# Last self attention of a twelve-stage decoder kernel: ScalarE's exponentials of a unit ahead of its casts of the next group's queries

## The chip, the cores and the metric

One core of a Trainium2 chip runs the whole program in one launch. The metric is the device time in microseconds. The kernel before took 1790.76 us in the median of three runs (1790.09, 1790.76, 1799.61). The program is four decoder layers of three sublayers each (self attention, cross attention or a stand-in for it, feed-forward), on a residual of 4 batches of 256 tokens of 256 features.

## The reference

The change lies in the self attention of the last layer: 16 heads of 16 features, causal, on the layer-normalised residual. The other eleven sublayers are the same in both kernels.

```python
def _L3_attn_ref(x, w_qkv, b_qkv, w_out, b_out):
    qkv = x @ w_qkv + b_qkv
    q, k, v = jnp.split(qkv, 3, axis=-1)
    q, k, v = (heads(q), heads(k), heads(v))        # b, 16 heads, 256 tokens, 16
    scores = jnp.einsum('bhql,bhkl->bhqk', q, k) / math.sqrt(HEAD)
    scores = jnp.where(q_ind < k_ind, jnp.float32(-10000.0), scores)
    probs = jax.nn.softmax(scores, axis=-1)
    combined = jnp.einsum('bhqk,bhkl->bhql', probs, v)
    combined = combined.transpose(0, 2, 1, 3).reshape(b, s, HIDDEN)
    return combined @ w_out + b_out

x = x + _L3_attn_ref(_layernorm(x, axis=-1), ...)
```

## The kernel before

Each of twelve stages is a function (`l0_attention` to `l3_ffn`) that returns five Python generators, one for each engine's queue: TensorE `t`, VectorE `v`, ScalarE `a`, GpSimd `g`, SyncE `sp`. The order in which a generator issues instructions is the order in that engine's queue. `yield signal, key` asks for the count of a semaphore at which a step is done, and `wait_ge` on it makes the engine wait; every instruction behind it in the same queue waits too. `yield MEET` is a barrier of all engines. One stands at the end of the stage `l3_attention` and at its beginning.

The stage works on 16 groups m of four heads in one batch (group m has batch m // 4), each of two units of two heads: unit u belongs to group u // 2, and there are UNITS = 32. All five generators run over the same iterations n = 0 to 41 (`LAST = UNITS + 10`), and in iteration n each engine does its step for a unit that is some iterations behind. There is no other scheduler: the order inside an iteration is written out by hand.

The queries and keys are split into three bf16 parts whose sum carries the float32 value. A pair of iterations begins a group: in the even iteration n the group n // 2 is projected (`qkv_tensor` on TensorE, L101) and moved out of PSUM with its bias (`qkv_vector` on VectorE, L2779 and L2780). ScalarE casts the first part of the queries in the same even iteration, the second part in the odd one and the third part in the next even one (`parts_scalar`, L2579, called with 0, 1 and 2); VectorE casts the keys likewise (`parts_vector`, L2569), and after each cast GpSimd takes the part from what is left (`parts_gpsimd`, L2586 and L2588), for which the next cast waits.

For unit u the steps are, with the iteration in which each is issued:
- n = u + 3: TensorE turns the parts of queries and keys (`narrow_turns_tensor`, L107, bf16 identity). VectorE copies an odd unit's result (L2881) in the same iteration, ScalarE an even unit's (L2920).
- n = u + 4: TensorE makes the scores of both heads (`narrow_scores_tensor`, L2616, L2617 and L2619; L2617 fills the masked block). The scores of the units go round three PSUM banks, so the second head of unit u needs the bank that the first head of unit u - 1 held, and waits until its exponentials are done (`score_bank_free` with the signal `exped`). VectorE masks and takes the maxima (`masked_maxima`, L2842, L2844, L2846, the last being the negated maximum). ScalarE takes the exponentials, four instructions with their sums (`exponentials_scalar`, L585, waiting for `neg_max`, and for a buffer and the sums of earlier units).
- n = u + 5: VectorE inverts the sums (`sums_vector`, L597), GpSimd multiplies (`shares_gpsimd`, L605).
- n = u + 6: TensorE turns the shares (`share_turns_tensor`, L107, float32 identity). In n = u + 7 VectorE copies the first head's (L543) and ScalarE the second head's (L550).
- n = u + 8: TensorE multiplies with the values (`heads_tensor_of_pair`, L2800). For an even unit of a later group it first waits for ScalarE's copy of the group before (`heads_copied`, L2808, issued in the even iteration 2m + 10).
- For each batch, in n = 17, 25, 33 and 41, TensorE makes the output product (L101) and VectorE adds it to the residual (L403) and takes statistics.

Besides these, VectorE works for the next stage in n = 9, 13 (its weights as integers) and 21, 29, 37 (its activations), ScalarE copies weights in n = 12 and 16 (L2731, L2732) and normalises a batch in n = 19, 27 and 35 (L367), for which GpSimd has made the scale in n = 18, 26 and 34 (L328 to L340).

TensorE's order in an iteration is: turns of n - 3, scores of n - 4, heads of n - 8, projection (even n), output product, turns of the shares of n - 6. VectorE's: copy of the shares' turn, copy of the queries' turn (even n), maxima, inverted sums, cast of the third part (even n), projection's bias (even n), cast of the first or second part, output, work for the next stage.

Of the kernel before, what the change touches and what calls it, by code (L numbers as in the profile page):

```python
# [44 lines left out]
UNITS = GROUPS * NB * 2  # L45
# [85 lines left out]
def build(nc, d, out):  # L131
# [442 lines left out]
    def exponentials_scalar(A, n, src_of=score_bank):  # L574
        k = n % 2
        for hh in range(2):
            e, src = A.eb[(2 * n + hh) % len(A.eb)], src_of(n, hh)
            a.wait_ge(*(yield neg_max, A.s, n, hh))
            if n >= A.depth:
                a.wait_ge(*(yield p_in_psum, A.s, n - A.depth, hh))  # L580
            if n >= 2:
                a.wait_ge(*(yield vs, A.s, "sums", n - 2))
            for i in range(TB):
                c = slice(A.ko[i], A.ko[i] + A.kw[i])
                ins = a.activation(e[:, c], src[:, c], ACT.Exp, bias=A.mx[k][:, 2 * hh + i:2 * hh + i + 1], scale=A.scale,  # L585
                                   accum_out=A.ls[k][:, 2 * hh + i:2 * hh + i + 1])
            ins.then_inc(*exped.up(A.s, n, hh))
# [1984 lines left out]
    def parts_scalar(N, m, n):  # L2572
        cur, q5 = N.current(m, n), slots(N.qx[m % 2])
        if n:
            a.wait_ge(*(yield rest_of, N.A.s, m, n - 1))
        lo, hi = Q_SLOTS[n]
        for i in range(TB):
            src = cur[:, i, 0:64].rearrange("p (h o c) -> p h o c", h=HG, o=1)
            ins = a.copy(q5[:, i, :, lo:hi, :], src.broadcast_to([P, HG, hi - lo, HD]))  # L2579
        ins.then_inc(*part_a.up(N.A.s, m, n))  # L2580
# [153 lines left out]
    def l3_attention():  # L2734
# [10 lines left out]
        A = Attention(s, BF16, HD, HD ** -0.5, False, outs=(), q_cols=1024, depth=3)  # L2745
# [156 lines left out]
        def scalar():  # L2902
            yield from norm_scalar(s, nf, None, [3], both=True)
            for n in range(LAST):
                if n == 1:
                    yield from turned_scalar(s, 3, heads_bank)
                if n - 3 in WEIGHTS:
                    yield from cross_weights_scalar(A, WEIGHTS.index(n - 3))
                if n in (19, 27, 35):
                    yield from norm_scalar("l3x", cross_nf, None, [(n - 19) // 8], both=True)  # L2910
                if 0 <= n - 10 < UNITS and n % 2 == 0:
                    yield from heads_copied((n - 10) // 2)
                if 0 <= n - 7 < UNITS:
                    yield from probability_turns_scalar(A, n - 7)
                if 0 <= n - 3 < UNITS and n % 2:
                    u = n - 3
                    a.wait_ge(*(yield q_in_psum, s, u))
                    if u >= 2:
                        a.wait_ge(*(yield scored, s, u - 2, 1))
                    a.copy(*narrow_turned(N, u)).then_inc(*q_t_a.up(s, u))  # L2920
                if 0 <= n - 1 < UNITS and n % 2 == 0:
                    yield from parts_scalar(N, n // 2 - 1, 2)
                if n < UNITS and n % 2 == 0:
                    a.wait_ge(*(yield vs, s, "qkv", n // 2))
                    yield from parts_scalar(N, n // 2, 0)
                if n < UNITS and n % 2:
                    yield from parts_scalar(N, n // 2, 1)
                if 0 <= n - 4 < UNITS:
                    yield from exponentials_scalar(A, n - 4)
            yield MEET  # L2930

        def gpsimd():
# [406 lines left out]
```

## Time and profile before

| what | value |
|---|---|
| runs before | 1790.09, 1790.76, 1799.61 us; median 1790.76 |
| the profiled execution | 1797.26 us |
| its span, first to last instruction | 1795.9 us |
| instructions | 27080 |
| mean granted TensorE clock | 0.85 of full |
| busy in the whole span | TensorE 1496.4 us (83%), VectorE 1144.2 (64%), ScalarE 818.3 (46%), GpSimd 765.6 (43%) |

The stage of the change runs from about 1226 us of the span, where its pipeline begins, to about 1432 us, where the next stage's first instructions follow the barrier. The shares of busy time in the table are means over twelve stages with different limits and say little on this one.

In the profile's rows PE is TensorE, DVE is VectorE, ACT is ScalarE, POOL is GpSimd. L585 is line 585 of the kernel. A row of a timeline is an instruction or several like it, and in brackets the idle time of the engine ahead of it, with what ended that time; "issue" stands where no releaser is seen.

### The profile page before, as it was taken

Reading aid. Unit: us, or ns where it says so; the run is one execution under the profiler, and the core shown is the slowest. Engines: PE = TensorE matmul, PEld = TensorE weight load, DVE = VectorE, ACT = ScalarE, POOL = GpSimd, SP = SyncE. Lnnn points to the kernel's source line nnn. Section 1 sums busy time; section 2 is a strip of 40 time slices with the busy share of each in tenths; the row PEclk is TensorE's granted clock in tenths of the full one; section 3 lists DMA queues with packets and bytes.
Section 4 is the critical chain, followed back from the end, with each engine's and each line's share of the span. In section 5 each row is a group of like instructions: output and inputs, shape, how many; then the busy total and the mean of one; then the engine's idle time right before and its main releaser. Section 6 shows DMA issues by size and latency. Waiting matters only on the chain. (4 is left out here: it accounts for less than half of the span.)

```text
span 1795.9 us, 27080 instructions
## 1 busy us (share of the span) xinstructions
PE 1496.4 (83%) x8792; PEld 1110.0 (62%) x8792; DVE 1144.2 (64%) x2987; ACT 818.3 (46%) x2138; POOL 765.6 (43%) x1199
## 2 busy tenths in 40 slices
PE   3899997899999948999898694166777689959999
PEld 3567673578888822333476584035555479958888
DVE  2577786255555569988555526886888579963222
ACT  1244443134444338887515313456665468832111
POOL 3388882046555646666422204275455322220000
PEclk8799997799999975555599897587989879968999
DMA  5100000200000025555420000200000020000000
GB/s 218 56 7 7 1 2 12 100 14 6 7 1 1 1 53 92 95 89 94 123 99 1 1 1 27 84 16 1 1 1 1 35 108 2 2 1 1 7 6 12
DMA packets 98379, 62.21 MB, mean 35 GB/s; under 512 B 88896, under 2 KB 93376, under 8 KB 96448
## 3 DMA queue, kind: packets, MB, share of 16 engines
q1 hardware_dynamic: 98240, 60.48, 12.6%
q8 instruction: 72, 1.18, 0.3%
q14 instruction: 67, 0.55, 0.1%
HBM read 38.44 MB, written 1.05 MB: 22 GB/s over the span
## 5 line engine op out<-in xcount | busy, mean ns | idle before, releaser
L101 PE MATMUL banks<-normed_t,arena_a 128*128 128x256 f32 x1120 | 258.9, 387 | 3.0 <-PEq L3244 3.0
L101 PEld LDWEIGHTS banks<-normed_t,arena_a 128*128 128x128 f32 x1120 | 217.1, 195 | 34.7 <-issue 4.1
L446 POOL TENSOR_TENSOR lut_weights<-lut_weights,arena_b 128x536 f32<-128x536 f32 x128 | 179.5, 1402 | 123.8 <-DVE arena_b L436 114.0
L605 POOL TENSOR_SCALAR work<-work,small 128x256 f32<-128x256 f32 (+1 forms) x384 | 175.5, 475 | 85.5 <-DVE small L597 85.2
L101 PE MATMUL banks<-arena_a 64*128 64x512 bf16 (+1 forms) x384 | 161.6, 540 | 30.8 <-PEq L3244 18.7
L1615 ACT ACTIVATE arena_a<-banks,work 128x1024 uint8<-128x1024 f32 x128 | 154.1, 1205 | 47.1 <-DVE work L1553 40.5
L1551 DVE TENSOR_REDUCE work<-banks 128x1 f32<-128x1024 f32 x128 | 155.3, 1214 | 24.3 <-PE banks L101 24.3
L1645 POOL TENSOR_SCALAR arena_a<-arena_a 128x1024 bf16<-128x1024 uint8 x128 | 132.2, 1045 | 65.1 <-DMA arena_a<-arena_a 64.6
L107 PE MATMUL banks<-identity,work 128*128 128x128 f32 x968 | 136.9, 283 | 19.4 <-ACT work L550 7.4
L585 ACT ACTIVATE work<-banks,small 128x256 f32<-128x256 f32 (+1 forms) x258 | 115.3, 458 | 62.5 <-DVE small L572 58.7
L107 PEld LDWEIGHTS banks<-identity,work 128*128 128x128 f32 x968 | 116.2, 149 | 34.8 <-POOL work L605 12.7
L1741 DVE TENSOR_TENSOR big_b<-big_b,banks 128x512 f32<-128x512 f32 (+2 forms) x48 | 30.8, 642 | 148.2 <-PE banks L101 128.0
L328 POOL TENSOR_SCALAR rstd<-mean_var 128x2 f32<-128x2 f32 x48 | 10.1, 209 | 245.3 <-DVE mean_var L399 163.5
L1757 ACT ACTIVATE big_b<-banks 128x512 f32<-128x512 f32 (+2 forms) x48 | 26.7, 560 | 176.7 <-PE banks L101 176.6
L101 PEld LDWEIGHTS bank<-work,arena_a 128*128 128x128 bf16 x1024 | 37.2, 106 | 110.8 <-POOL arena_a L1645 75.7
L101 PE MATMUL banks<-arena_a,normed_t 128*128 128x192 f32 (+2 forms) x320 | 100.2, 465 | 3.5 <-PEq L3244 3.5
L2579 ACT CAST big_a<-big_b 128x192 bf16<-128x192 f32 (+1 forms) x192 | 55.3, 340 | 76.6 <-DVE big_b L2779 48.3
L101 PE MATMUL bank<-big_b,work 128*128 128x16 f32 (+2 forms) x596 | 84.4, 279 | 0.4 <-DVE work L543 0.3
L101 PEld LDWEIGHTS banks<-arena_a,normed_t 128*128 128x128 f32 x320 | 58.5, 217 | 36.9 <-issue 35.9
L101 PEld LDWEIGHTS bank<-big_b,work 128*128 128x128 f32 x596 | 75.2, 198 | 5.7 <-DVE work L543 3.9
L101 PE MATMUL bank<-arena_a,big_b 128*128 128x256 f32 x288 | 70.2, 388 | 4.6 <-DVE big_b L2035 2.8
L101 PEld LDWEIGHTS banks<-arena_a 64*128 64x128 bf16 (+1 forms) x384 | 39.6, 134 | 55.3 <-issue 35.2
(403 smaller groups left out, 3401.9 us busy)
## 6 DMA issues: line engine op xcount, KB each, us to landing
arena_a<-in_L3f_wg SPq DMA_DIRECT2D x1, 4096.0 KB, 12.6
arena_b<-in_lut_idx SPq DMA_DIRECT2D x8, 268.0 KB, 3.2
arena_b<-in_L_wqn SPq DMA_DIRECT2D x1, 2048.0 KB, 12.0
arena_b<-in_L_wo SPq DMA_DIRECT2D x1, 2048.0 KB, 17.8
arena_a<-in_L_wq SPq DMA_DIRECT2D x1, 2048.0 KB, 7.6
arena_a<-in_L_wo SPq DMA_DIRECT2D x1, 2048.0 KB, 13.0
arena_a<-arena_a SPq DMA_TRANSPOSE x128, 2.5
arena_b<-in_L2f_gv SPq DMA_DIRECT2D x1, 2048.0 KB, 8.3
```

Of the source, the lines that this page charges most:

```text
L101: ins = t.matmul(out, lhs_t, rhs, start=start and i == 0, stop=stop and i == n - 1)
L107: ins = t.transpose(out, src, ident[0:src.shape[0], 0:src.shape[0]])
L328: g.tensor_scalar(dst, src, factor, more, ALU.mult, ALU.add).then_inc(*gs.up())
L446: g.tensor_tensor(o, o, lut_t[j % 2], ALU.add).then_inc(*summed.up(c * LUT + j))
L585: ins = a.activation(e[:, c], src[:, c], ACT.Exp, bias=A.mx[k][:, 2 * hh + i:2 * hh + i + 1], scale=A.scale, accum_out=A.ls[k][:, 2 * hh + ...
L605: ins = g.tensor_scalar(e[:, c], e[:, c], A.rl[n % 2][:, 2 * hh + i:2 * hh + i + 1], 0.0, ALU.mult, ALU.add)
L1551: v.tensor_reduce(mx[:, z:z + 1], wide[n % 3], AX.X, ALU.max).then_inc(*vs.up())
L1615: a.activation(eb[n % 6].bitcast(U8), wide[n % 3], ACT.Exp, bias=mx[:, n:n + 1], scale=sq[:, n:n + 1], accum_out=ls[:, n:n + 1]).then_inc( ...
L1645: g.tensor_scalar(pt[n % 6].rearrange("p (j e q) -> p j e q", j=NT // 2, e=2), by_byte(p8[n % 6]), 1.0, 0.0, ALU.mult, ALU.add).then_inc(* ...
L1741: ins = v.tensor_tensor(o[r, cols], o[r, cols], (banks[q % 3 * 2].f if r.start else up)[r, cols], ALU.mult)
L1757: ins = a.activation(F.hidden(q)[dst, cols], banks[q % 3 * 2].f[src, cols], ACT.Silu)
L2579: ins = a.copy(q5[:, i, :, lo:hi, :], src.broadcast_to([P, HG, hi - lo, HD]))
```

## The change

In ScalarE's generator of this stage, in every iteration, the exponentials of unit n - 4 move from the end of the iteration to a place ahead of the cast of the first part (even n, with its wait for VectorE's projection) or of the second part (odd n). They stay behind the copies of turned shares and queries and behind the cast of the third part. No instruction, wait, buffer or DMA is added or taken away, and the other engines' queues are as they were.

```diff
@@ -2920,13 +2920,13 @@
                     a.copy(*narrow_turned(N, u)).then_inc(*q_t_a.up(s, u))
                 if 0 <= n - 1 < UNITS and n % 2 == 0:
                     yield from parts_scalar(N, n // 2 - 1, 2)
+                if 0 <= n - 4 < UNITS:
+                    yield from exponentials_scalar(A, n - 4)
                 if n < UNITS and n % 2 == 0:
                     a.wait_ge(*(yield vs, s, "qkv", n // 2))
                     yield from parts_scalar(N, n // 2, 0)
                 if n < UNITS and n % 2:
                     yield from parts_scalar(N, n // 2, 1)
-                if 0 <= n - 4 < UNITS:
-                    yield from exponentials_scalar(A, n - 4)
             yield MEET
 
         def gpsimd():
```

ScalarE's queue in n = 22 and 23 (L2808, L550, L2579 x32: copy of the heads, copy of the shares' turn, cast of the third part; then L2579 x48, first part, L585, the exponentials of unit 18; from the second L550 on n = 23), before:

```order
L2808 COPY big_a<-bank 128x256
L550 COPY work<-banks 128x512
L2579 CAST big_a<-big_b 128x4x32 x2
L2579 CAST big_a<-big_b 128x4x48 x2
L585 ACTIVATE work,small<-banks,small 128x256 x4
L550 COPY work<-banks 128x512
L2920 COPY work<-banks 128x1024
L2579 CAST big_a<-big_b 128x4x48 x2
L585 ACTIVATE work,small<-bank,small 128x256 x2
L585 ACTIVATE work,small<-banks,small 128x256 x2
```

and with the change:

```order
L2808 COPY big_a<-bank 128x256
L550 COPY work<-banks 128x512
L2579 CAST big_a<-big_b 128x4x32 x2
L585 ACTIVATE work,small<-banks,small 128x256 x4
L2579 CAST big_a<-big_b 128x4x48 x2
L550 COPY work<-banks 128x512
L2920 COPY work<-banks 128x1024
L585 ACTIVATE work,small<-bank,small 128x256 x2
L585 ACTIVATE work,small<-banks,small 128x256 x2
L2579 CAST big_a<-big_b 128x4x48 x2
```

In both iterations the row L585 and the cast L2579 128x4x48 have changed places: in n = 22 the exponentials are behind the third part's cast, in n = 23 behind the copy of the turned queries (L2920), and the heads' copy of n = 24, which comes next in the queue, now follows the cast of the second part.

ScalarE's queue in n = 4 and 5, the first iterations with exponentials, before:

```order
L2579 CAST big_a<-big_b 128x4x32 x2
L2579 CAST big_a<-big_b 128x4x48 x2
L585 ACT_TABLE_LOAD
L585 ACTIVATE work,small<-banks,small 128x256 x4
L2920 COPY work<-banks 128x1024
L2579 CAST big_a<-big_b 128x4x48 x2
L585 ACTIVATE work,small<-bank,small 128x256 x2
L585 ACTIVATE work,small<-banks,small 128x256 x2
```

and with the change:

```order
L2579 CAST big_a<-big_b 128x4x32 x2
L585 ACT_TABLE_LOAD
L585 ACTIVATE work,small<-banks,small 128x256 x4
L2579 CAST big_a<-big_b 128x4x48 x2
L2920 COPY work<-banks 128x1024
L585 ACTIVATE work,small<-bank,small 128x256 x2
L585 ACTIVATE work,small<-banks,small 128x256 x2
L2579 CAST big_a<-big_b 128x4x48 x2
```

The load of the table for the exponential moves with the first of them, ahead of the cast of group 2's first part.

## Rows read from the trace of the kernel before

**Rows 1.** Waits of ScalarE, 1226 to 1414 us: total us, times, longest
```profile
ACT big_a L2579 <- DVE big_b L2779: 48.3, 15, 5.7
```

**Rows 2.** Waits of VectorE, 1226 to 1414 us, same columns
```profile
DVE residual L403 <- PE banks L101: 6.7, 3, 2.4
...
DVE work L2881 <- PE banks L107: 5.7, 6, 2.3
...
DVE big_b L2779 <- PE banks L101: 4.9, 4, 3.0
```

**Rows 3.** Windows: us; busy us (count) of PE, PEld, DVE, ACT, POOL; clock; DMA
```profile
1236.00:1414.00 178.00, 135.09 (x1050) 97.99 (x1050) 148.98 (x422) 115.06 (x397) 91.70 (x191) 0.89 0.00 1
...
1370.00:1382.00 12.00, 10.28 (x75) 7.28 (x73) 8.09 (x24) 7.78 (x30) 3.59 (x9) 0.72 0.00 0
```

**Rows 4.** Timeline, n = 22 to 24: start us, duration us, engine, line, operation
```profile
1338.38 0.17 DVE L2846 TENSOR_SCALAR small<-small 128x2 f32<-128x2 f32 x1
...
1339.65 0.17 DVE L2846 TENSOR_SCALAR small<-small 128x2 f32<-128x2 f32 x1
...
1340.26 0.61 PE L107 MATMUL banks<-identity_bf,big_a 128*128 128x128 bf16 x8 [1.40 <-issue]
...
1340.52 0.61 ACT L2579 CAST big_a<-big_b 128x192 bf16<-128x192 f32 x2 [4.05 <-DVE big_b L2779]
...
1341.03 0.47 ACT L585 ACTIVATE work<-banks,small 128x256 f32<-128x256 f32 x1
...
1342.10 0.23 PE L2616 MATMUL banks<-work 128*128 128x128 bf16 x1 [1.02 <-ACT work L585]
...
1342.84 0.59 ACT L550 COPY work<-banks 128x512 f32<-128x512 f32 x1
...
1344.21 0.64 ACT L2579 CAST big_a<-big_b 128x192 bf16<-128x192 f32 x2
...
1344.25 0.17 DVE L2846 TENSOR_SCALAR small<-small 128x2 f32<-128x2 f32 x1
...
1344.61 1.92 POOL L605 TENSOR_SCALAR work<-work,small 128x256 f32<-128x256 f32 x4 [1.72 <-DVE small L597]
...
1345.28 0.69 DVE L543 COPY work<-banks 128x512 f32<-128x512 f32 x1 [0.45 <-PE banks L107]
...
1346.53 0.42 ACT L2808 COPY big_a<-bank 128x256 f32<-128x256 f32 x1
...
1346.62 0.69 DVE L2881 COPY work<-banks 128x1024 bf16<-128x1024 bf16 x1 [0.65 <-PE banks L107]
```

**Rows 5.** Timeline, VectorE, its other waits in the stage
```profile
1240.03 0.43 DVE L2842 COPY_PREDICATED banks<-arena_b 128x256 f32<-128x256 int32 x1 [1.68 <-PE banks L2619]
...
1278.29 0.43 DVE L2779 TENSOR_TENSOR big_b<-banks,arena_a 128x256 f32<-128x256 f32 x1 [1.10 <-PE banks L101]
...
1298.37 0.69 DVE L543 COPY work<-banks 128x512 f32<-128x512 f32 x1 [2.20 <-PE banks L107]
...
1357.20 0.69 DVE L403 TENSOR_TENSOR residual<-banks,residual 128x512 f32<-128x512 f32 x1 [2.35 <-PE banks L101]
...
1377.25 0.42 DVE L2779 TENSOR_TENSOR big_b<-banks,arena_a 128x256 f32<-128x256 f32 x1 [3.03 <-PE banks L101]
...
1394.22 0.69 DVE L543 COPY work<-banks 128x512 f32<-128x512 f32 x1 [0.61 <-PE banks L107]
```

**Rows 6.** Timeline, ScalarE and TensorE: the start, n = 15 and n = 25
```profile
1236.39 0.60 ACT L2579 CAST big_a<-big_b 128x192 bf16<-128x192 f32 x2 [2.02 <-DVE big_b L2779]
...
1237.01 1.28 ACT L585 ACT_TABLE_LOAD   x1
...
1239.38 0.29 PE L2616 MATMUL banks<-work 128*128 128x128 bf16 x1 [2.43 <-ACT work L585]
...
1293.44 0.29 PE L2616 MATMUL bank<-work 128*128 128x128 bf16 x1 [0.40 <-ACT work L585]
...
1352.13 0.23 PE L2616 MATMUL banks<-work 128*128 128x128 bf16 x1 [0.94 <-ACT work L585]
```

## Prediction

> **What bounds the kernel now.** The change touches one stage, the last self attention, from about 1226 to 1432 us of the span. It is a software pipeline of 42 iterations (n = 0 to 41), and no engine is full in it: between 1236 and 1414 us VectorE is busy 149.0 of 178 us (84%), TensorE's matmuls 135.1, ScalarE 115.1, GpSimd 91.7 [rows 3]. So the stage goes at the pace of VectorE plus whatever VectorE waits for. I read the waits in two views. ScalarE waits longest at its first cast of a group's queries, for VectorE's projected queries: 15 times, 48.3 us [rows 1]. That is the wait in front of the moved exponentials, but idle time of an engine with a third to spare costs nothing by itself. VectorE's own list is what counts: 6.7 us for the output products (L403), 5.7 us for turned queries (L2881), 4.9 us for projections (L2779), all behind TensorE [rows 2].
>
> The timeline of n = 22 to 24 shows how the two lists hang together [rows 4]. VectorE has negated the maxima of the even unit's two heads at 1338.55 and 1339.82. ScalarE sits in the cast's wait (4.05 us) until 1340.52, starts the first exponential at 1341.03 and only then frees a score bank; TensorE waits 1.02 us for that (1342.10), and comes late to the heads, the turned shares and the turned queries. VectorE waits for these two turns: 0.45 us at 1345.28 and 0.65 us at 1346.62.
>
> **What the change does to one pair.** The four exponentials of a unit (1.81 us, 1341.03 to 1342.84, accumulator reads in it [rows 4]) go ahead of the cast. Nothing is added or removed; no DMA, no queue of SP and nothing on GpSimd moves. Even iteration: first head from 1338.55 to about 1339.45, second from 1339.82 to 1340.72, inside the 4.05 us. The cast then starts at 1340.72 instead of 1340.52, 0.2 us late. It feeds GpSimd's remainder, and GpSimd is busy with shares at that time, as it is at 1344.61 in the row of the odd iteration, so I cost it at nothing. TensorE's second head finds its bank free: its 1.02 us is gone.
>
> Odd iteration: ScalarE's copies (L550, 1342.84 before) come some 1.6 us sooner. The exponentials now stand ahead of the cast of the second parts, and wait for the maxima, ready at 1344.42 for the second head. They end at 1345.3, and the cast (0.64 us, from 1344.21 before) at about 1345.9 instead of 1344.85: a full microsecond later. Its cover is GpSimd, which forms shares from 1344.61 to 1346.53 and can't take the remainder sooner [rows 4]; 0.6 us of cover is left. Without that cover each microsecond would go on to the third cast and to the exponentials behind it. The heads' copy (L2808) comes at 1345.85 instead of 1346.53, 0.7 us sooner, and TensorE's heads and next projection wait for it.
>
> What is late next is VectorE itself: from 1339.65 to 1344.25 it works through without a wait [rows 4]. So a pair gains at most what VectorE waited, and where it did not wait, nothing.
>
> **The sum**, wait by wait:
> - n = 22 to 24: VectorE waited 0.45 + 0.65 = 1.10; TensorE's chain comes 1.02 sooner: **1.0 us** [rows 4].
> - n = 30 to 32: 0.61 at 1394.22, under the same 1.02: **0.6 us** [rows 5].
> - The output products of the first three batches: VectorE waits 2.35 at 1357.20 behind scores (0.94 of wait at 1352.13), heads and 16 output matmuls. Batches 0 and 1 have this wait on the exponentials, batch 2 comes after the last cast of queries: 2 x 0.94 = **1.9 us** [rows 5, 6].
> - n = 16, at 1298.37: 2.20 of wait, of which TensorE lost 0.40 (at 1293.44) to the exponentials: **0.4 us** [rows 5, 6].
> - n = 12, at 1278.29: 1.10 for a projection behind the heads' copy, which comes 0.7 sooner: **0.7 us** [rows 4, 5].
> - The start, n = 4 and 5: the first exponentials stand behind the cast and a table load (1.28 us from 1237.01), TensorE waits 2.43 at 1239.38 and VectorE 1.68 at 1240.03 [rows 5, 6]. ScalarE had been free from 1234.37 (2.02 us idle ahead of the cast at 1236.39). In the new order the load starts there and ends at 1235.7, the first head's exponentials at 1236.6, before TensorE begins to wait (1239.38 less 2.43 is 1236.95): **1.7 us**.
> - VectorE's longest waits at L2881 (up to 2.3) follow iterations where ScalarE first waits for the next stage's normalisation [rows 2]. That one runs on GpSimd behind the shares, and the change does not bring it forward: nothing. The same for 3.03 at 1377.25, which comes after such an iteration: nothing. After the last group nothing changes.
>
> Together 6.3 us. The profiled execution took 1797.26 us, 6.5 more than the median of the runs, 1790.76; from it the sum gives 1791.0, and against the median **1784.5 us** (0.35% less). The clock of TensorE is the unknown cost. Bounds from rows: at best every wait of VectorE in the lists goes, 17.3 us in the three groups of [rows 2] and 4.9 more at 1240.03, 1298.37, 1345.28 and 1394.22 [rows 4, 5], 22 us in all; at worst none goes and new ones come, of the size of the two long ones, 2.20 and 3.03 [rows 5]. I take neither, because in the pair of rows 4 VectorE's wait is no longer than the wait of TensorE that goes.
>
> The row of the table load weighs against a page: the load takes 1.28 us and the exponential follows within 0.1 us of its end, as TensorE's wait for it until 1239.38 bears out [rows 6]. The Trainium skill, "ScalarE: Activation LUTs", section "What ACT_TABLE_LOAD costs", adds a drain of about 1.38 us, 2.66 in all. By that figure, as an estimate from the page, the first head's exponentials would end 1.4 us later, at 1238.0 instead of 1236.6, TensorE would wait 1.05 instead of 2.43, the start would gain 1.4 instead of 1.7, and the sum would be 6.0. The trace shows no such drain here.
>
> **Rivals.**
> *The clock gains too.* From 1370 to 1382 us the mean granted clock is 0.72, against 0.89 in the stage [rows 3]: TensorE was at 1.2 GHz for over half of that stretch and VectorE waited 3.03 us in it; the 2.20 at 1298.37 is of the same kind [rows 5]. In rows 4 TensorE has two gaps, 1.40 and 1.02 us, within 2 us. If taking one away keeps it at 2.4 GHz, both long waits go: 3.03 and the 1.80 left of the other, 4.8 us more, 11.1 in all, **1779.7 us**. For it: gaps go. Against: a pipeline paced by VectorE leaves TensorE its idle time, only elsewhere.
> *Absorbed.* VectorE's total work sets the pace, the heads' copy now follows the second head's maxima and the cast, and the next wait (projection, remainder) takes what is won, except at the start: 1.7 us, **1789 us**. For it: several pairs have no wait of VectorE at all. Against: 0.7 us less until the heads' copy.
> *Slower.* TensorE gets ahead, and its idle time falls together into one gap in front of the heads, where it waits for the heads' copy; it then falls to 1.2 GHz in pairs that kept 2.4 GHz, and the heads and the projection run late, as at 1377.25. It decides once more than two pairs of the 14 do so, since each costs 2.20 to 3.03 us [rows 5] against 6.3 of gain; with six pairs 6 x 2.6 = 15.6 less 6.3 is 9.3 lost, **1800 us**. For it: one long gap in place of two short. Against: the heads' copy comes sooner than now, and there are gaps of this size already.
> The Trainium skill, "TensorE: Matmul & The Clock Gate", section "What's actually happening", says that the default state is throttled and that activity releases the throttle. By that rule the last rival would hold where gaps merge and the first where they shrink; the trace agrees only in that the clock is below full here, and can't say which it will be.
>
> **How the numbers follow.** Forecast 0.47, clock gains 0.22, absorbed 0.24, slower 0.07. The range reaches from a little under the clock rival, 1777, to no gain at all with a median some 3 us towards the slowest run shown (1799.6): 1794. About 0.5%, 9 us here, is what a measurement of this kernel can tell from no change; the bounds are 1781.8 and 1799.7. Under 1781.8: the clock rival nearly whole (0.20) and the lower part of the forecast (0.13), 0.33. Over 1799.7: the slower rival and a trace of the absorbed, 0.08. The rest, 0.59, within.
>
> **What would show it.** In the changed profile ScalarE's wait of 48.3 us for L2779 should fall to under 20 and partly turn into waits for the maxima (L2846); TensorE's waits for the exponentials at L2616 of about 1 us should go; VectorE's first wait at L2842 (1.68) should go, its waits at L403 shrink to about 1.4 in two batches; the stage should be about 6 us shorter and all others the same. The prediction is wrong if VectorE's busy time in the stage grows, if new waits of 2 us and more stand at L2779 or L2881, if ScalarE's third cast waits long for GpSimd (L2588), or if the granted clock in the stage leaves 0.86 to 0.92.

## The result, and the profile after

| | before | after |
|---|---|---|
| median of 20 runs each | 1794.26 us | 1789.47 us |
| lowest and highest | 1790.09 to 1799.61 | 1784.33 to 1792.62 |
| ratio after / before, 95% interval | | 0.9973 [0.9964, 0.9982] |
| span of the profiled execution | 1795.9 us | 1787.6 us |
| mean granted clock | 0.850 | 0.855 |

The change gains 0.27%, 4.8 us, well clear of nothing and within the half per cent. The median of the kernel before is that of all 20 runs; the three shown ahead of the prediction had 1790.76.

How much of it lies in the stage? I measured the stage on VectorE, from the start of its first integers of the next stage's weights (L2870) to the start of the last output batch (L403). That took 207.9 us before and 203.3 after: 4.66 us shorter. The two profiled spans differ by 8.3 us; of the remaining 3.6 us, 2.1 lie ahead of the stage and 1.5 behind it, where the two kernels issue the same instructions. So the stage's 4.66 us, not the 8.3, is to be explained, and it agrees with the medians.

The waits of the changed kernel between 1222 and 1410 us, first ScalarE's (engine, tile and line that waits, engine and line it waits for; us in total, times, longest):

```profile
ACT work L585 <- DVE small L2846: 30.2, 40, 3.7
ACT big_a L2579 <- POOL big_b L2588: 9.8, 12, 1.8
ACT arena_a L367 <- POOL tiny L340: 9.3, 3, 3.2
ACT big_a L2579 <- DVE big_b L2779: 6.2, 4, 2.3
```

The 48.3 us for the projection [rows 1] are 6.2, and 30.2 us are now waits for the maxima. The change does what it says. Longer than before is the third line: ScalarE comes to the next stage's normalisation (L367) earlier and waits 9.3 us in three waits for its scale; before, the same three came to 6.0 us (1.57, 1.57 and 2.85). The second line grew as well: the casts that wait for GpSimd (L2588) waited 4.2 us before and 9.8 now, 1.8 at most. TensorE's list, same window:

```profile
PE bank L2800 <- ACT big_a L2808: 13.9, 10, 2.2
PE banks L107 <- ACT work L550: 10.3, 3, 3.5
PE banks L2616 <- ACT work L585: 3.1, 5, 1.5
```

The waits for a score bank (L2616) fell from 19.2 us in 22 places to 3.4 in 6. In their stead TensorE waits in front of the heads (L2800) for ScalarE's copy of the heads, 13.9 us against 6.8 before, and in front of the turned shares (L107 for L550) 10.3 against 7.4. (The figures of before are those from 1222 to 1416 us, where the same instructions lie.) VectorE's list, which sets the pace:

```profile
DVE big_b L2779 <- PE banks L101: 9.8, 4, 3.6
DVE residual L403 <- PE banks L101: 4.8, 3, 2.0
DVE work L2881 <- PE banks L107: 4.8, 3, 2.6
```

Against [rows 2] the output products went from 6.7 to 4.8 and the turned queries from 5.7 to 4.8. The waits for the projection grew. Their 9.8 us contain the wait for the very first projection of the stage (2.2 us, and 2.0 before), which lies ahead of the window of [rows 2]; without it they went from 4.9 to 7.7. The window that answers to the first of [rows 3], with the same distances from the two ends of the stage (same columns):

```profile
1233.90:1407.30 173.40, 132.89 (x1050) 100.01 (x1050) 149.02 (x421) 116.74 (x396) 92.99 (x193) 0.90 0.01 1
```

VectorE is busy the same 149.02 us (149.0 before), but in 173.4 us instead of 178: 85.9% instead of 83.7%. The clock is 0.90 against 0.89.

**Pair by pair.** One pair of iterations runs from one projection (L2779 on VectorE) to the next. The 15 distances in both traces, laid against the terms of the prediction, with what VectorE's own waits show:

| place | predicted gain, us | measured, us |
|---|---|---|
| start, n = 4 to 8 | 1.7 | 1.85 |
| n = 12 | 0.7 | -0.6 |
| n = 16 | 0.4 | 1.7 |
| output of batch 0 (n = 17) | 0.94 | 1.05 |
| n = 20, after a normalisation | 0 | -1.7 |
| n = 24 | 1.0 | 1.0 |
| output of batch 1 (n = 25) | 0.94 | 0.8 |
| n = 28, after a normalisation | 0 | -0.3 |
| n = 32 | 0.6 | 1.0 |
| all other pairs | 0 | -0.2 |
| sum | 6.3 | 4.6 |

(The rows are rounded; the stage is 4.66 us shorter.) Five of the seven priced terms came out within 0.4 us. Three places carry the difference: n = 12 and n = 20 lose 1.3 and 1.7 us against the prediction, n = 16 wins 1.3. All of this is read from one profiled execution of each kernel.

**The start** is as the prediction had it, here ScalarE's first exponentials and VectorE's second head in n = 4 and 5:

```profile
1232.23 1.28 ACT L585 ACT_TABLE_LOAD   x1
1233.52 0.47 ACT L585 ACTIVATE work<-banks,small 128x256 f32<-128x256 f32 x1
...
1236.39 0.42 DVE L2842 COPY_PREDICATED banks<-arena_b 128x256 f32<-128x256 int32 x1
```

The table is loaded 2.7 us sooner, counted from the start of the stage (12.2 us after it instead of 14.9), in time in which ScalarE stood idle before, and the exponential starts 0.01 us after the load's end, in this order too; no drain is seen. The 1.68 us of VectorE's wait at L2842 [rows 5] are gone.

**n = 12**, where the heads' copy was to come 0.7 us sooner and did, and the pair still became longer:

```profile
1270.45 0.40 ACT L2808 COPY big_a<-bank 128x256 f32<-128x256 f32 x1
...
1271.00 1.06 PE L2800 MATMUL bank<-work,big_b 128*32 128x256 f32 x8 [2.25 <-ACT big_a L2808]
...
1271.98 2.86 PE L101 MATMUL banks<-arena_a,normed_t 128*128 128x192 f32 x8
...
1274.88 0.42 DVE L2779 TENSOR_TENSOR big_b<-banks,arena_a 128x256 f32<-128x256 f32 x1 [1.92 <-PE banks L101]
```

TensorE no longer waits for the score bank, so it arrives early at the heads, and its idle time there is one piece of 2.25 us. The projection that follows runs in 2.86 us; at the full clock it takes 1.57. The mean granted clock is 0.52 from 1272.00 to 1274.84 us, which is TensorE at 1.2 GHz for nearly all of it; before, the heads and the projection of this place ran at 1.00 (1275.70 to 1278.30 us), which is 2.4 GHz. The gap alone doesn't decide it: in this same trace a gap of 1.73 us in front of the heads is followed by a projection of 2.88 us at n = 10 and by one of 1.57 at n = 22 and at n = 30. VectorE's wait went from 1.10 [rows 5] to 1.92.

**n = 20**, behind the normalisation of a batch in n = 19:

```profile
1314.58 1.09 ACT L367 ACTIVATE arena_a<-residual,tiny,rstd 128x256 f32<-128x256 f32 x2 [3.20 <-POOL tiny L340]
...
1316.28 0.93 PE L107 MATMUL banks<-identity,work 128*128 128x128 f32 x4 [3.39 <-ACT work L550]
...
1318.10 0.69 DVE L2881 COPY work<-banks 128x1024 bf16<-128x1024 bf16 x1 [2.63 <-PE banks L107]
...
1319.79 1.92 PE L2800 MATMUL bank<-work,big_b 128*32 128x256 f32 x8 [0.87 <-ACT big_a L2808]
1321.64 2.36 PE L101 MATMUL banks<-arena_a,normed_t 128*128 128x192 f32 x8
...
1324.04 0.42 DVE L2779 TENSOR_TENSOR big_b<-banks,arena_a 128x256 f32<-128x256 f32 x1 [2.15 <-PE banks L101]
```

The same place before:

```profile
1320.59 1.09 ACT L367 ACTIVATE arena_a<-residual,tiny,rstd 128x256 f32<-128x256 f32 x2 [1.57 <-POOL tiny L340]
...
1325.81 1.06 PE L2800 MATMUL bank<-work,big_b 128*32 128x256 f32 x8 [0.66 <-ACT big_a L2808]
...
1326.80 1.57 PE L101 MATMUL banks<-arena_a,normed_t 128*128 128x192 f32 x8
...
1328.40 0.42 DVE L2779 TENSOR_TENSOR big_b<-banks,arena_a 128x256 f32<-128x256 f32 x1 [0.56 <-PE banks L101]
```

ScalarE's queue stands behind L367 for 3.20 us (1.57 before), and L550, the copy that TensorE wants, is behind it. TensorE waits 3.39 us in one piece instead of 1.04. This wait is longer because TensorE comes sooner, and not because the copy comes later: from L367 to the heads it is 5.21 us now and was 5.22 before. The loss lies behind that. The heads take 1.92 us instead of 1.06 and the projection 2.36 instead of 1.57, together 1.65 of the 1.70 us by which the pair is longer. The mean granted clock over the two is 0.58 (1319.79 to 1324.00 us); before it was 1.00. VectorE's wait for the projection is 2.15 us; before it was 0.56. In both kernels TensorE is at 1.2 GHz for 6.8 us from about 96.5 us behind the start of the stage; before, the heads of n = 20 began at 103.7, behind this stretch, and now they begin at 99.7, in it.

**n = 16** shows the same thing with the other sign. The stretch at 1.2 GHz around it is 3.4 us long instead of 6.8 in the trace's record of the clock, and VectorE's 2.20 [rows 5] became 0.38:

```profile
1293.27 0.69 DVE L543 COPY work<-banks 128x512 f32<-128x512 f32 x1 [0.38 <-PE banks L107]
```

Where these stretches fall differs from kernel to kernel. The kernel with the even half of the change alone (below) took 0.78 us less than before at n = 12, with a projection of 1.57 us, and only 0.6 less at n = 16.

So the traces say where the time went, and at n = 20 that two slow products carry it, but not what another order or another clock would give. Two theories stood after them. **Order:** ScalarE's queue holds copies that TensorE needs (L2808, L550) behind things that come late, and moving these copies gives time back. **Clock:** what costs is the 1.2 GHz behind TensorE's gaps. A third was that the gain of the change is in one of its two halves alone.

### The profile page after: what moved, and what is told of

It reads as the page before. It is cut to its first block and busy times, and to the rows that moved or that the text cites. A ratio compares the mean times of both kernels' runs of the same rounds, so it can differ in the third digit from the quotient of the medians.

```text
span 1787.6 us, 27080 instructions
## 1 busy us (share of the span) xinstructions
PE 1486.9 (83%) x8792; PEld 1107.4 (62%) x8792; DVE 1144.1 (64%) x2987; ACT 821.5 (46%) x2138; POOL 768.4 (43%) x1199
## 3 DMA queue, kind: packets, MB, share of 16 engines
HBM read 38.44 MB, written 1.05 MB: 22 GB/s over the span
## 5 line engine op out<-in xcount | busy, mean ns | idle before, releaser
L107 PE MATMUL banks<-identity,work 128*128 128x128 f32 x968 | 135.5, 282 | 23.5 <-ACT work L550 10.3
L585 ACT ACTIVATE work<-banks,small 128x256 f32<-128x256 f32 (+1 forms) x258 | 115.1, 453 | 79.1 <-DVE small L572 58.9
L107 PEld LDWEIGHTS banks<-identity,work 128*128 128x128 f32 x968 | 115.1, 148 | 38.1 <-POOL work L605 18.7
L328 POOL TENSOR_SCALAR rstd<-mean_var 128x2 f32<-128x2 f32 x48 | 10.1, 209 | 244.5 <-DVE mean_var L399 163.2
L101 PE MATMUL banks<-arena_a,normed_t 128*128 128x192 f32 (+2 forms) x320 | 104.4, 481 | 3.5 <-PEq L3244 3.5
L101 PE MATMUL banks<-arena_a,big_a 128*128 128x256 f32 x320 | 72.8, 380 | 1.1 <-ACT big_a L2808 0.6
```

Source lines behind the costliest of these rows:

```text
L101: ins = t.matmul(out, lhs_t, rhs, start=start and i == 0, stop=stop and i == n - 1)
L107: ins = t.transpose(out, src, ident[0:src.shape[0], 0:src.shape[0]])
L328: g.tensor_scalar(dst, src, factor, more, ALU.mult, ALU.add).then_inc(*gs.up())
```

## The experiments

All kernels were timed in five rounds beside the kernel before on the same chip. "Stage" is the length defined above, from each kernel's one profiled execution; before has 207.9, the change 203.3.

### Even iterations alone, odd iterations alone

The exponentials are moved only in even n, ahead of the cast of the first part:

```diff
+                if 0 <= n - 4 < UNITS and n % 2 == 0:
+                    yield from exponentials_scalar(A, n - 4)
                 if n < UNITS and n % 2 == 0:
                     a.wait_ge(*(yield vs, s, "qkv", n // 2))
...
-                if 0 <= n - 4 < UNITS:
+                if 0 <= n - 4 < UNITS and n % 2:
                     yield from exponentials_scalar(A, n - 4)
```

> Only the even iterations have the exponentials ahead of the cast (first part); the odd ones keep the old order. Theory W (VectorE sets the pace, and the change pays where TensorE's second head of scores no longer waits for the exponentials behind ScalarE's wait for the projection): the whole gain is here, 3.5 to 6 us under before, within 1 us of the full change. Rival O (the odd half pays, since there the exponentials come sooner and free the banks for the even units): 0 to 2 us under before. Rival C (the gain is luck of TensorE's clock): anything between -3 and +6 us, and no relation to the full change.

Measured: 1788.14 against 1793.47 us, 0.9973 [0.9959, 0.9987]; stage 203.1. And with the exponentials moved in odd n alone:

> Only the odd iterations have the exponentials ahead of the cast (second part); the even ones keep the old order. Theory W: 0 to 1 us under before, TensorE's waits of about 1 us for the exponentials at L2616 and the 1.7 us of VectorE at the start still there. Rival O: 3 to 5 us under before. A cost of the odd half (the cast of the second part is late for GpSimd) would show as 1 us or more over before.

Measured: 1793.59 against 1793.47 us, 0.9994 [0.9979, 1.001]; stage 205.3. The even half has the whole gain, and the odd half can't be told from nothing. What it did in its single profile (2.6 us) does not show in the medians, so I take nothing from it. Its profile has 37.5 us at 1.2 GHz in the stage, where the kernel before has 51.2 and the change 47.8, so the time doesn't simply follow that sum either. At n = 20, where the change lost 1.70 us, the kernel with the even half lost 2.09, again with the heads at 1.92 and the projection at 2.78 us: this loss is in two kernels.

### The heads' copy earlier (on the change)

```diff
-                if 0 <= n - 10 < UNITS and n % 2 == 0:
-                    yield from heads_copied((n - 10) // 2)
...
+                if 0 <= n - 9 < UNITS and n % 2:
+                    yield from heads_copied((n - 9) // 2)
                 if 0 <= n - 4 < UNITS:
                     yield from exponentials_scalar(A, n - 4)
```

The copy of the heads stood at the start of iteration 2m + 10; now it stands in 2m + 9, ahead of the exponentials.

> The full change, and the copy of the heads (L2808) taken from the beginning of the even iteration 2m+10 to the odd iteration 2m+9, ahead of the exponentials and behind the copy of the turned queries. Theory H (after the change the heads' copy behind exponentials and cast is what TensorE waits for, 13.9 us in ten waits, and it merges TensorE's idle time into one gap in front of the heads, so that the projection runs late and at the lower clock): that wait falls under 3 us, VectorE's waits at L2779 fall from 9.8 to under 5, and the time is 3 to 5 us under that of the full change, 8 to 10 under before. Rival V (VectorE's own work is all that bounds it now): within 1 us of the full change.

Measured: 1782.89 against 1793.47 us, 0.994 [0.9919, 0.9961]; stage 196.8. TensorE's waits for L2808 are gone. VectorE's list (1222 to 1410 us):

```profile
DVE work L2881 <- PE banks L107: 4.6, 4, 2.1
...
DVE big_b L2779 <- PE banks L101: 4.3, 4, 1.9
```

The waits for the projection fell from 9.8 to 4.3, and the pair that ends at n = 12 from 10.97 to 10.28. By the medians that is some 5.9 us under the change, a little more than expected. TensorE was at 1.2 GHz for 47.8 us of the stage, as long as in the change, so the 6.5 us of the stage came without less of the low clock. They did not come without a change in its places: the projections of n = 12, 20 and 28 ran in 1.57 us each here, and in 2.86, 2.36 and 2.86 in the change. This run doesn't part order from clock; the one with the projection ahead of the heads does.

### The normalisation later (on the change)

`if n in (19, 27, 35): yield from norm_scalar("l3x", ...)` goes from the top of ScalarE's iteration to its end, behind the cast of the second part; nothing else moves.

> The full change, and the next stage's normalisation on ScalarE (L367, n = 19, 27, 35) taken from the head of its iteration to its end. If its wait for GpSimd (9.3 us in three waits) holds up the copy of the shares' turn and with it TensorE (10.3 us) and VectorE (4.8 us at L2881): TensorE's wait for L550 falls under 2 us, VectorE's at L2881 under 1.5, and the time is 3 to 5 us under that of the full change. If something else is late there (GpSimd's shares, the clock): under 1.5 us.

Measured: 1785.36 against 1793.47 us, 0.9953 [0.9935, 0.9971]; stage 199.2. From the list of TensorE's waits in this kernel:

```profile
PE bank L2800 <- ACT big_a L2808: 19.9, 11, 2.9
```

and from VectorE's:

```profile
DVE big_b L2779 <- PE banks L101: 11.1, 5, 3.1
...
DVE work L2881 <- PE banks L107: 0.2, 1, 0.2
```

The wait behind L550 is gone, and so is VectorE's for the turned queries, 4.8 to 0.2. But the next item in the queue behind the normalisation is now the heads' copy, and TensorE waits for it up to 2.9 us; the waits for the projection grew from 9.8 to 11.1. The wait has moved by one place. Against the change it is some 3.6 us, as expected.

### Both moves (on the change)

> The full change with both further moves on ScalarE: the copy of the heads ahead of the odd exponentials, and the next stage's normalisation at the end of its iteration. If the two waits are separate, their gains add: about 5.8 + 3.4, so 14 us under before (ratio 0.992 or less), and VectorE has hardly a wait over 1 us left but the output products. If the second only uncovers what the first hides (the clock, the shares): not more than 1 us under the run with the heads' copy alone.

Measured: 1774.05 against 1794.1 us, 0.9887 [0.9868, 0.9906]; stage 187.3. These are 20 us, where the expectation had 14. VectorE's waits:

```profile
DVE residual L403 <- PE banks L101: 10.1, 4, 5.7
...
DVE big_b L2779 <- PE banks L101: 1.5, 1, 1.5
DVE work L2881 <- PE banks L107: 0.4, 2, 0.2
```

And ScalarE in the timeline around the first normalisation:

```profile
1317.81 1.09 ACT L367 ACTIVATE arena_a<-residual,tiny,rstd 128x256 f32<-128x256 f32 x2
1318.80 0.57 ACT L550 COPY work<-banks 128x512 f32<-128x512 f32 x1
```

L367 has no idle time ahead of it any more, since GpSimd's scale is there when ScalarE arrives. The 1.5 us at L2779 are the first projection's; no later one is waited for. (The list's 10.1 us at L403 include the last batch's 5.7, which starts before 1410 us in this kernel.) The distances between projections from n = 18 on are 8.96, 11.50, 8.98, 11.79, 8.96, 11.50: the short ones have no work beside the pair's own, the long ones have the next stage's or an output batch. The change had 13.96, 11.61, 9.04, 12.15, 14.47, 11.61 there. TensorE was at 1.2 GHz for 27.3 us instead of 47.8.

### The same two moves without the change

The heads' copy earlier on the kernel before:

> The kernel before (exponentials at the iteration's end), with only the heads' copy moved to the odd iteration behind the copy of the turned queries. Theory H with the change as a condition (before it, TensorE waited for the exponentials first, so an early heads' copy finds TensorE late anyway, 6.8 us of waits of which VectorE felt little): 1 to 4 us under before. If the heads' copy is independent of the change: 5 to 7 us under before, as between the full change and the run with the heads' copy.

Measured: 1790.87 against 1794.1 us, 0.9986 [0.9972, 0.9999]; stage 205.0, within the 1 to 4 us. The normalisation later on the kernel before:

> The kernel before, with only the next stage's normalisation on ScalarE (L367) moved to the end of its iteration. The prediction held that its wait is independent of the change. If so: 3 to 4 us under before, as between the full change and the run with the normalisation moved (0.9973 to 0.9953). If it only counts once the exponentials are out of the way: 0 to 1.5 us under before.

Measured: 1784.26 against 1795.64 us, 0.9941 [0.9928, 0.9953]; stage 199.5. That is 10.6 us by the ratio, far more than either expectation allowed. The pairs that end at n = 20 and n = 28 went from 12.26 to 10.59 and from 14.18 to 10.59. The heads and the projection of n = 28, before:

```profile
1372.75 1.92 PE L2800 MATMUL bank<-work,big_b 128*32 128x256 f32 x8 [0.66 <-ACT big_a L2808]
...
1374.60 2.62 PE L101 MATMUL banks<-arena_a,normed_t 128*128 128x192 f32 x8
```

and in this kernel, with VectorE's wait:

```profile
1368.68 1.06 PE L2800 MATMUL bank<-work,big_b 128*32 128x256 f32 x8 [1.06 <-ACT big_a L2808]
...
1369.67 1.57 PE L101 MATMUL banks<-arena_a,normed_t 128*128 128x192 f32 x8
...
1371.28 0.42 DVE L2779 TENSOR_TENSOR big_b<-banks,arena_a 128x256 f32<-128x256 f32 x1 [0.49 <-PE banks L101]
```

VectorE's wait was 3.03 [rows 5]. At n = 20 the two products ran at the full clock in both kernels, so the 1.67 us there are the queue's: ScalarE's wait for GpSimd, with L550 behind it. At n = 28 the gain is 3.59 us. The same 1.67 are in it, and the other 1.91 are the two products, which ran in 1.06 and 1.57 us instead of 1.92 and 2.62. So the long wait had both causes, and the later normalisation took both away. Both moves on the kernel before:

> The kernel before with both further moves (heads' copy, normalisation), but without the change itself. Against 0.9887 with it, this tells what the change is worth once its two successors are out of the way. If the waits are in series (removing one shows the next): 0.995 to 0.997, so that the change alone is worth 0.6 to 0.8%. If they are separate sums: 0.991 to 0.993, the change worth 0.3% as when alone.

Measured: 1782.05 against 1795.64 us, 0.9932 [0.9912, 0.9951]; stage 197.1. The ratio lies just over the 0.991 to 0.993 expected for separate sums. Its stretches at 1.2 GHz are 47.8 us long, as in the change. VectorE's list now has waits that the change would take away:

```profile
DVE work L543 <- PE banks L107: 7.1, 6, 2.1
DVE residual L403 <- PE banks L101: 6.7, 3, 2.4
...
DVE banks L2842 <- PE banks L2619: 2.0, 2, 1.6
```

Put together, as ratios to the kernel before:

| | heads' copy and normalisation as before | heads' copy early | normalisation late | both |
|---|---|---|---|---|
| without the change | 1 | 0.9986 | 0.9941 | 0.9932 |
| with the change | 0.9973 | 0.994 | 0.9953 | 0.9887 |
| what the change brings | 0.27% | 0.46% | -0.12% | 0.45% |

The last row is the quotient of the two above it. In the last three columns the two kernels ran on different chips, each beside its own runs of before. With intervals of some 0.2% on each ratio, the -0.12% is no measured loss, while the 0.45% under "both" is larger than nothing; it can't be told from the 0.27% of the change alone. The heads' copy is worth 0.14% by itself and 0.33% on the change (0.994 / 0.9973), two values that the intervals don't part. Two differences are larger than the intervals. The change and the late normalisation together bring 0.47%, and not 0.86%; and the heads' copy brings 0.66% on top of these two (0.9887 / 0.9953), and not 0.14%. So these don't add. The three together bring 1.13%, and their single gains add up to 1.00%, which is the same within the noise.

### The projection ahead of the heads (on the change)

```diff
+                if n < UNITS and n % 2 == 0:
+                    yield from qkv_tensor(n // 2)
                 if 0 <= n - 8 < UNITS:
                     yield from heads_tensor_of_pair(n - 8)
-                if n < UNITS and n % 2 == 0:
-                    yield from qkv_tensor(n // 2)
```

This is TensorE's queue. It leaves the late copy late, and takes only the projection out from behind it.

> The full change, and on TensorE in the even iterations the next group's projection ahead of the heads instead of behind them; ScalarE as in the full change. Theory H: the gap in front of the heads (waits of up to 2.25 us for L2808) is filled with 1.6 us of the projection, VectorE's waits at L2779 (9.8 us) go to under 1, and the time is 3 to 5 us under that of the full change. Rival V (VectorE's own work): within 1 us of the full change.

Measured: 1784.42 against 1794.1 us, 0.9952 [0.9935, 0.997]; stage 197.6. Without the first projection of the stage (1.9 us here, ahead of the window), the waits at L2779 fell from 7.7 us to 0.2, with a clock of 0.88 between 1224 and 1410 us. The time is 0.21% under the change's, some 3.8 us. The projection of n = 20 was still slow here, as was that of n = 28 (2.53 us), and VectorE waited for neither:

```profile
1316.37 2.45 PE L101 MATMUL banks<-arena_a,normed_t 128*128 128x192 f32 x8
```

So a projection at the lower clock is not waited for where it doesn't stand behind the heads and their wait for L2808. The pair of n = 20 became 3.0 us shorter by that and the next one 0.9 longer. The waits for the turned shares (10.3 us for L550) are as in the change, as they should be, since nothing on ScalarE has moved.

### Work in TensorE's gap (on the change)

Ahead of the heads of every even n from 8 on, 20 bf16 matmuls of the identity with itself, into the bank that the projection then overwrites. They add no result; they fill the gap. `bank_of` is the wait for that bank, which the projection did before (its lines are left out).

```diff
...
+        def fill_tensor(m):
+            yield from bank_of(m)
+            for _ in range(20):
+                t.matmul(A.bank01["q", m].f[:, 0:P], id_b, id_b, start=True, stop=True)
...
+                if 8 <= n < UNITS and n % 2 == 0:
+                    yield from fill_tensor(n // 2)
                 if 0 <= n - 8 < UNITS:
                     yield from heads_tensor_of_pair(n - 8)
```

> The full change, and in the even iterations from n = 8 on 20 small bf16 matmuls (1.1 us at 2.4 GHz) ahead of the heads, into the bank that the projection overwrites next; their results are read by nobody, the output is as before. They fill part of TensorE's gap without doing anything of use, so only the clock can gain. If the lower clock after the gap is what makes the projection late (2.86 us instead of 1.57 at n = 12): granted clock in the stage from 0.89 to 0.93 or more, VectorE's waits at L2779 from 9.8 to under 6, 1 to 3 us under the full change. If the clock doesn't follow that gap: clock as it was, and 0 to 8 us over the full change, as much as the added work is not hidden.

Measured: 1786.49 against 1794.1 us, 0.9968 [0.9953, 0.9983]; stage 202.5. The filling did change the clock: TensorE was at 1.2 GHz for 37.5 us instead of 47.8 (0.92 of full between 1224 and 1410 us, where 0.93 had been expected), and at n = 12 the projection ran in 1.57 us instead of 2.86 (the lines are the fill, the heads and the projection):

```profile
1267.56 1.29 PE L2767 MATMUL banks<-identity_bf 128*128 128x128 bf16 x20 [0.26 <-ACT arena_b L2732]
1268.78 1.06 PE L2813 MATMUL bank<-work,big_b 128*32 128x256 f32 x8
1269.77 1.57 PE L101 MATMUL banks<-arena_a,normed_t 128*128 128x192 f32 x8
```

The wait of VectorE for it (now line 2792) was 0.85 us instead of 1.92 and the pair 0.4 us shorter; without the first projection, the sum of these waits fell from 7.7 to 5.0. At n = 20 it is plainer still:

```profile
1317.59 1.06 PE L2813 MATMUL bank<-work,big_b 128*32 128x256 f32 x8
1318.58 1.57 PE L101 MATMUL banks<-arena_a,normed_t 128*128 128x192 f32 x8
```

Both products are back at the full clock, with TensorE's wait for L550 ahead of them unchanged (3.39 us), and the pair is 12.87 us instead of 13.96; it was 12.26 before. All of the 1.65 us is back, and the filling, which ends behind the heads' copy, costs 0.6 of it again. In the time of the kernel it can't be told from the change (0.9968 and 0.9973, each within the other's interval). In the profile, what n = 12, 20 and 28 gave back (2.4 us) was mostly lost again at n = 16 and 18 and behind the last projection (2.0 us). So the clock explains the losses at n = 12 and n = 20, and a filling that itself takes TensorE's time is no way to cash them.

### Everything, and the even half with the two moves

> The change, the early heads' copy, the late normalisation, and the projection ahead of the heads on TensorE. The heads' copy and the projection's place cure the same gap (each took TensorE's waits for L2808 away), so with the copy early the projection's place should add little: 0.985 to 0.989 of before, against 0.9887 for the run without it. If the two are separate gains: 0.982 to 0.985.

Measured, the change with the heads' copy early, the normalisation late and the projection ahead: 1770.72 against 1795.64 us, 0.9863 [0.9847, 0.988]; stage 187.3, the same as without the projection's move. The even half with the two moves on ScalarE:

> As the run with both further moves, but with the exponentials ahead of the cast in the even iterations only. If the odd half is still worth nothing: within 1.5 us of that run (0.9887 of before). If the odd half matters once ScalarE's other waits are gone (the exponentials of the odd unit free the bank for the next even one): 2 to 4 us over it; if its late cast costs there: 1 to 3 us under it.

Measured: 1776.02 against 1795.64 us, 0.9893 [0.9876, 0.991]; stage 186.4. Both ratios are as expected. Nothing is left of the odd half here either. The best kernels are these last ones and the one with both moves; the intervals of 0.9863 and 0.9887 overlap, so I name no winner between them.

## Why the prediction was right in kind and wrong in size

- **The mechanism held.** ScalarE's 48.3 us became 6.2 and waits for the maxima; most of TensorE's waits for the score bank went, and VectorE's first one at L2842; L403 shrank to 1.30 and 1.51 in two batches; the stage is shorter and the clock stays at 0.90. The terms for the start (1.7, measured 1.85), n = 24 (1.0 and 1.0), the two output batches (1.9 and 1.85) and n = 32 (0.6 and 1.0) came out as worked. The even half alone brings the whole gain. The odd iterations, with their late cast that the prediction took for covered, neither gain nor lose by themselves.
- **The step that failed in n = 12**: "n = 12, at 1278.29: 1.10 for a projection behind the heads' copy, which comes 0.7 sooner: 0.7 us". The copy came 0.65 us sooner. But the projection took 2.86 instead of 1.57 us, 1.3 more, since TensorE was at 1.2 GHz in it. The term was -0.6. With the gap in front of it filled, the projection was back at 1.57.
- **The step that failed in n = 20**: "That one runs on GpSimd behind the shares, and the change does not bring it forward: nothing." GpSimd's scale did not come sooner, as said, and ScalarE's queue behind it kept its distances (5.2 us from L367 to the heads in both kernels). What the 0 left out is TensorE's clock, "the unknown cost", in the heads and the projection that follow. They ran at 1.2 GHz instead of 2.4 and took 1.65 us more; the measured term is -1.7. At n = 28, where the two products had been slow already, it is -0.3. By the prediction's own list this was a sign of being wrong: a new wait of 2 us and more at L2779, here 2.15 where 0.56 had been.
- **The 0.4 at n = 16** was too small (1.7), because the 1.80 that I had left to the clock rival went as well. So the clock rival was right in this place, the slower rival in the other two. By this count the clock's part is +1.3 at n = 16, -1.3 at n = 12 and -1.7 at n = 20, which is the whole difference between 6.3 and 4.6. That the sum came out so near is luck in part, since n = 16 and n = 12 cancel. With the even half alone n = 12 gained 0.78 and n = 16 only 0.6, at the same time for the whole kernel. The prediction put these rivals against each other as if one of them had to hold everywhere.
- **The base.** I took the sum off the median of three runs, 1790.76, though its profiled execution was already 6.5 us above it. The median of 20 is 1794.26, 3.5 us higher. The forecast of 1784.5 is therefore 5.0 us from the measured 1789.47 while the sum is off by 1.5 (6.3 against 4.8). The range, 1777 to 1794, held it, and the change lies within half a per cent, as was held likeliest.
- **The 3.03 at n = 28** stood in the sum as a wait behind the normalisation and in the clock rival as a matter of the clock. It was both: with the normalisation later it fell to 0.49 us, and of the 3.59 us that this pair gained, 1.67 are the queue's and 1.91 the clock's.
- The Trainium skill, "ScalarE: Activation LUTs", section "What ACT_TABLE_LOAD costs", would have had the start gain 1.4 by the prediction's estimate from it. It gained 1.85, and in both orders the exponential follows the load within 0.1 us.

What stays open: what decides where TensorE's stretches at 1.2 GHz fall, since gaps of the same length were followed by either clock; how far the figures of single pairs hold beyond the one profiled execution of each kernel; and why the odd half is shorter in one profile and not in the medians.

## What to carry to other kernels

In a pipeline of in-order queues, ask of every wait that is taken away where its engine stops next: here TensorE ran on to two copies that stood in ScalarE's queue behind something late, and 2.6 us of 7.4 were given back in the pairs behind them, nearly all of it as products at the lower clock. Put a copy that another engine waits for ahead of the work that itself waits, and put work for a later stage, whose input comes late, at the end of the iteration. Such moves need not add: measure them together before one is dropped for bringing little (the heads' copy was worth 0.14% alone and 0.66% on top of the change and the late normalisation).

## What the runs showed of the hardware

With the same instructions, TensorE's heads took 1.06 or 1.92 us and the projection 1.57 or 2.86 us, at a mean granted clock of 1.00 or of 0.52 to 0.58. The length of the gap in front of them did not foretell which: 1.73 us were followed by 2.88 us at n = 10 and by 1.57 at n = 22 and n = 30. Nor did the kernel's time follow the sum of the low clock: 37.5 us of it in the stage came with a ratio of 0.9994 (the odd half alone), 47.8 us with 0.994 (the change with the early heads' copy). That 20 small matmuls without a result bring the projection back to 1.57 us I had hoped for; that the kernel gains nothing measurable by it, I had not expected. The Trainium skill, "TensorE: Matmul & The Clock Gate", section "What's actually happening", says that activity releases the throttle; the filled kernel agrees, with 37.5 us at 1.2 GHz against 47.8, though the odd half alone had 37.5 us without any filling.
